# The messages of a graph layer: the scaling and shift of v on GpSimd in place of ScalarE

## What is computed

```python
z = jnp.concatenate([node_feats[src], node_feats[dst], edge_feats], axis=1)
z = z @ W.T + b                                    # 256 columns an edge
mean = jnp.mean(z, axis=0)
var = jnp.mean(jnp.square(z - mean), axis=0)
z = (z - mean) * jax.lax.rsqrt(var + BN_EPS) * gamma + beta
msg = jax.nn.sigmoid(z[:, :H]) * jax.nn.softplus(z[:, H:])
agg = jnp.zeros_like(node_feats).at[src].add(msg)
return node_feats + agg
```

## Time and profile before

| | us |
|---|---|
| median of 3 runs | 4397.55 |
| lowest and highest | 4392.38, 4400.34 |
| the profiled execution | 4391.44 |
| its span in the trace | 4389.2 |
| PE busy | 3005.1 (68%) |
| DVE busy | 2808.1 (64%) |
| POOL busy | 2540.0 (58%) |
| ACT busy | 2214.8 (50%) |

### The profile page before, as it was taken

How to read it: one execution, slowest core, us unless ns; L and a number is a source line. 1 busy time by engine, 2 the same in 40 slices (tenths; PEclk the granted TensorE clock), 3 DMA queues, 4 the chain that set the end, 5 groups by cost and what they waited for, 6 DMA issues and landing times. The chain is left out here.

```text
span 4389.2 us, 80992 instructions
## 1 busy us (share of the span) xinstructions
PE 3005.1 (68%) x17430; PEld 2153.3 (49%) x17431; DVE 2808.1 (64%) x7053; ACT 2214.8 (50%) x5936; POOL 2540.0 (58%) x2618
## 2 busy tenths in 40 slices
PE   6866989999989999999996576666233333333341
PEld 3422444444457777777775465666233333333330
DVE  5898989999965545555553788888434344343457
ACT  2412989889866666666664999997100000000011
POOL 0787777777757777777774000000477777777750
PEclk8998999999999999999998789888655655565555
DMA  6333333333348888888888544442322222222240
GB/s 131 120 91 94 107 101 99 101 101 99 97 123 264 263 263 263 263 263 261 262 264 204 204 175 189 186 173 96 64 52 52 53 52 52 52 53 52 52 30 29
DMA packets 311349, 598.09 MB, mean 136 GB/s; under 512 B 53534, under 2 KB 191943, under 8 KB 305575
## 3 DMA queue, kind: packets, MB, share of 16 engines
q0 software_dynamic: 96992, 228.88, 20.5%
q1 hardware_dynamic: 175480, 246.10, 18.1%
q10 hardware_dynamic: 38736, 121.78, 7.3%
HBM read 406.57 MB, written 189.99 MB: 136 GB/s over the span
## 5 line engine op out<-in xcount | busy, mean ns | idle before, releaser
L345 POOL DMA_INDIRECT rec_d<-arena x830 | 846.7, 1020 | 392.7 <-issue 360.4
L1254 POOL DMA_INDIRECT arena<-x_tab,arena x880 | 834.1, 948 | 323.1 <-issue 278.2
L784 POOL DMA_INDIRECT arena<-b_tab,arena x880 | 832.7, 946 | 304.5 <-issue 256.9
L1266 PE MATMUL psum<-arena 128*128 128x129 f32 x1760 | 413.4, 428 | 730.5 <-DMA arena<-x_tab,arena 717.9
L1266 PEld LDWEIGHTS psum<-arena 128*128 128x128 f32 x1760 | 383.3, 330 | 760.4 <-issue 760.4
L1291 DVE TENSOR_TENSOR arena<-psum,arena 128x129 f32 x880 | 257.5, 293 | 673.0 <-PE psum L1266 553.6
L717 PE MATMUL psum<-arena 128*128 128x440 f16 x3360 | 663.6, 351 | 8.6 <-ACT arena L432 8.4
L805 DVE TENSOR_TENSOR arena<-psum,arena 128x512 f32<-128x512 f32 x440 | 283.4, 686 | 549.7 <-DMA arena<-b_tab,arena 280.3
L897 PE MATMUL psum<-weT,arena 128*128 128x256 f32 x1760 | 547.8, 393 | 53.7 <-DVE arena L805 50.4
L1242 ACT ACTIVATE arena<-l_idx 128x8 int32 (+1 forms) x110 | 22.9, 208 | 1079.1 <-DMA arena<-x_tab,arena 1069.4
L432 ACT ACTIVATE arena<-arena 128x128 f16<-128x128 f16 x1680 | 561.7, 386 | 0.0
(11 more groups left out here) (203 smaller groups left out, 5205.4 us busy)
## 6 DMA issues: line engine op xcount, KB each, us to landing
z_d<-arena ACTq DMA_DIRECT2D x220, 512.0 KB
arena<-z_d SPq DMA_DIRECT2D x44, 2560.0 KB, 8.5
arena<-rec_d SPq DMA_DIRECT2D x220, 260.0 KB
arena<-in_edge_attr SPq DMA_DIRECT2D x83, 640.0 KB
arena<-b_tab,arena POOLq DMA_INDIRECT x880
arena<-x_tab,arena POOLq DMA_INDIRECT x880, 2.5
rec_d<-arena POOLq DMA_INDIRECT x831, 2.6
b_tab<-arena ACTq DMA_DIRECT2D x49, 128.0 KB
```

The costliest lines, as they stand in the source:

```text
L345: nc.gpsimd.indirect_dma_start(rec_rows, bass.IndirectOffsetOnAxis(e_idx[:, s, k:k + 1], 0), e_buf[:, s, k, :], None).then_inc(s_es[s], 16)
L784: nc.gpsimd.indirect_dma_start(bg[:, s, k, :], None, b_tab, bass.IndirectOffsetOnAxis(rec[:, s, k, H:H + 1].bitcast(I32), 0)).then_inc(s_b ...
L1254: nc.gpsimd.indirect_dma_start(xg[:, s, k, :], None, x1_tab, bass.IndirectOffsetOnAxis(gi[:, s, k:k + 1], 0)).then_inc(s_xg[s], 16)
L1266: last = nc.tensor.matmul(bank(4 * s + q)[:, a * 256:a * 256 + H + 1], hotg[:, s, 2 * q + a, :], xg[:, s, 2 * q + a, :], start=True, stop= ...
```

## The change

GpSimd gets a list in the messages block: for each chunk it waits for q of that chunk and then computes s v + t in place over the same 5 x 512 columns with one tensor_scalar, a multiplication and an addition with a scalar per partition. ScalarE's two operations a pair are gone; its wait for both q stays, now ahead of the first logarithm. VectorE's wait for `s_v` stays as it was.

```diff
+            @block.gpsimd
+            def _(pool):
+                def scaled(c, j, it):
+                    v = chunk_half(j, 1)
+                    pool.wait_ge(s_q, c + 1)
+                    settle(pool, s_turn)
+                    nc.gpsimd.tensor_scalar(v, v, bn_s[:, 1:2], bn_t[:, 1:2], ALU.mult, ALU.add).then_inc(s_v, 1)
+
+                chunks(pool, scaled)
+
...
                     for i in range(2):
-                        v = chunk_half(j + i, 1)
                         wait(act, s_q, c + (i + 1))
-                        nc.scalar.activation(v, v, ACT.Identity, bias=bn_t[:, 1:2], scale=bn_s[:, 1:2]).then_inc(s_v, 1)
-                    for i in range(2):
                         nc.scalar.activation(ex[:, i, :, :], ex[:, i, :, :], ACT.Ln, bias=stat[:, 6:7]).then_inc(s_lg, 1)
```

## The result

The change makes the kernel slower by 0.6%: 4423.03 us (median of 5 runs, 4415.92 to 4424.93) against 4397.19 us (5 runs), a ratio of 1.0059 with a 95% interval of 1.0044 to 1.0073, or +19 to +32 us. The profiled execution has a span of 4413.8 us, 24.6 more than before. The forecast was +46 us, with a range from -5 to +132; sign and mechanism came out as forecast, the size at a little over half.

A forecast was written before the change was run, and what follows sets the result against it. ScalarE was taken to bound the messages stage at 28.63 us a pair, VectorE 10% behind. 21 periods x (31.04 - 28.63) = +50.6 us, less 4.9 at the start, gave +45.7: 4443 us, range 4393 to 4530.

The forecast's parts named there:

- Step 1: ScalarE in the messages stage loses two scalings, 4.92 us a pair; at most 2.1 won, plus 4.9 once at the start.
- Step 2: ScalarE's wait ahead of the logarithm, for one less sigmoid, was already satisfied and costs nothing.
- Step 3: GpSimd's operation between second sigmoid and L1027 has 11.4 us of slack, so as a link it costs nothing.
- Step 4: GpSimd's tensor_scalar over 2560 columns takes 3.2 us, within bounds of 2.17 to 5.06 us.
- halved two-input rate: Alternative price of GpSimd's operation, half its two-input tensor_tensor time: 2.5 us.
- Step 5: VectorE stands while GpSimd runs, except for one add; its pair of chunks becomes 31.04 us.
- two small terms: In VectorE's pair: 0.60 us off for one add beside GpSimd; 1.30 us of TensorE waits hidden under the stalls.
- Rival A: VectorE's compares run on beside GpSimd, only operations with two SBUF inputs stall: -49 us, 4349 us; chance 0.16.
- Rival B: GpSimd's operation takes only 2.2 us, the stall eating ScalarE's gain: +2 us, 4400 us; chance 0.09.
- Rival C: Stalls lower TensorE's clock, adding 6.6 us of waits a pair, 138 us over the forecast; chance 0.03.

The follow-up runs named there:

- e2: e1 plus GpSimd's tensor_scalar over 2560 columns on a buffer of its own that nobody waits for: 4418.45 us, 1.0045 of the kernel before.
- e4: The change with GpSimd's operation cut into five pieces of 512 columns: 4397.01 us, 0.9999 of the kernel before.
- e8: The change with GpSimd's operation cut into ten pieces of 256 columns: 1.0051 of the kernel before, 1.0039 when run again.
- e3: e2 with a GpSimd memset of the 2560 columns in place of the tensor_scalar: 4407.35 us, 1.0025 of the kernel before.
- e1: The change without GpSimd's operation and VectorE's wait for it, v left unscaled: 4360.05 us, 0.9914 of the kernel before.
- e6: e1 with the scaling of v as a tensor_scalar on VectorE ahead of L1027: 1.0198 of the kernel before.
- e12: e2 with GpSimd's operation started at the end of L1027's operation, beside VectorE's multiplication, instead of after the sigmoid: 1.0011 of the kernel before.

## Why the prediction came out as it did

*Step 1, ScalarE stops being the bound:* right. VectorE's wait for the logarithm is gone but for the first of the stage, where it fell from 24.32 to 19.62 us, the 4.9 us reckoned (4.7).

*Step 2, the wait before the logarithm:* right, ScalarE is idle for 0.3 us in all before the logarithms, as before the change.

*Step 3, no cost as a link in the chain:* right, shown by e2, which has the cost without the link, and L1034 waited for GpSimd nowhere.

*Step 4, GpSimd's duration, was mis-sized:* 3.2 us forecast, 2.53 measured. This alone is 2 x 0.67 x 21 = 28 us too much. The halved two-input rate, named there and passed over for the middle of the bounds, gave the right 2.5 us, but by luck: the pieces of e4 and e8 show 0.84 ns a column and 0.33 us an operation, not 0.99 ns a column. 0.84 ns is the memset's rate, (5.37 - 2.23) / (6321 - 2560) = 0.835 ns from the earlier trace rows and e3. So the branch of step 4 in which an operation with one input pays once for what it costs over a memset had the right form, and only its 0.12 us was too small: 2.48 - 2.23 = 0.25 us. The estimate from the Trainium skill's line rate ("GPSIMD Engine Reference", Engine selection), 2.13 us, was 0.4 too short for the whole operation, but its 0.83 ns a column agrees with the 0.84. The one from the same page's 1.8 cycles (Elementwise — side-by-side cycle accounting), 3.84 us, was 1.3 too long.

*Step 5, VectorE stands while GpSimd runs:* right in kind, shown by e2 and by the rows of one meeting. Its two small terms were off in opposite directions. An operation costs 1.67 us, not its whole duration once and the duration less 0.60 the other time: of 2.53 us 0.86 are free on the mean, an add or a wait that would have been there anyway. With the measured duration the rule of step 5 gives 2 x 2.53 - 0.60 = 4.46 us a pair, and 3.33 were measured, 24 us too much over the stage. And the waits for TensorE did not go under the stalls; 28.0 us of idle time before the adds are left in the stage, 1.27 a pair, where they were forecast at zero, 27 us too little. These two cancel by luck, so that the miss of 25 us looks like that of the duration alone. With the measured numbers, the 1.67 and 1.27 read from this same trace, the step's sum closes: 25.24 + 2 x 1.67 + 1.27 = 29.85 us a pair. The trace has (3055.88 - 2429.14) / 21 = 29.84 between the first and the last L1034 of a pair's first chunk. 21 x (29.84 - 28.63) - 4.7 = +20.7, and the stage grew by 20.9.

The first and last of these rows:

```profile
2429.14 2.83 DVE L1034 SCALAR_TENSOR_TENSOR arena<-arena 128x2560 f32<-128x2560 f32 x1 [19.62 <-ACT arena L996]
...
3055.88 2.81 DVE L1034 SCALAR_TENSOR_TENSOR arena<-arena 128x2560 f32<-128x2560 f32 x1
```

One reading ahead of the steps was off and changed nothing: the 3.43 us before L1027 end the pair before the one that was added up. The wait that belongs to that pair is the next:

```profile
2715.70 2.82 DVE L1027 SCALAR_TENSOR_TENSOR arena<-arena 128x2560 f32<-128x2560 f32 x1 [2.07 <-ACT arena L989]
```

*Rival A, the compares run on:* false, the compares are what stands; the price of its outcome, -49 us, was also too good by 11, as e1 shows. *Rival B, no change:* near in duration (2.53 against 2.32 us) but outside it. *Rival C:* not as priced. The clock did fall, from 0.88 to 0.84, but the idle time before the adds is 28.0 us against 27.6; its price shows in e6.

The rule of the Trainium skill ("SBUF — State Buffer", Who interferes with whom), that the operation which issues second is blocked to the end of the first, holds in each meeting shown: the compares behind GpSimd, GpSimd behind the multiplication in e12, the free adds from PSUM. That a memset stops the compares (e3) agrees with it as well, as compares of the two-port kind; that they are of that kind was inferred from the rate of a longer tensor_scalar and not shown by itself. That longer one is stopped by a memset as well (4.99 us instead of 3.36, e2).

## What to carry to other kernels

An idle GpSimd is not free help for a VectorE that is nearly full: before moving work there, look for one place in the trace where the two run at once, and charge VectorE the operation's duration less what of VectorE's list can run beside it. Only then compare with the slack that the engine relieved leaves, here 28.63 - 27.09 = 1.5 us a pair against 3.3. If the work must go there, five pieces in place of one took back 26 us in one test, but ten did not, as each has a cost of its own. A start where VectorE would have waited anyway left the stage 24 us shorter in another, compared across groups of runs.

## What the runs showed of the hardware that was not expected

- A GpSimd memset, which reads nothing, stops VectorE's short tensor_scalar compares almost as a tensor_scalar does: four of them took 2.12 us instead of 0.86 (e3).
- Five pieces of 512 columns took 4.21 us on GpSimd where one operation over the 2560 took 2.52, while VectorE lost 1.03 us a chunk instead of 1.67 ((235.0 - 189.7) / 44): of GpSimd's 1.7 us more, 1.3 are also there beside an idle VectorE, 3.79 against 2.48 us (e4).
- GpSimd's tensor_scalar with two scalars per partition, beside no VectorE operation, took 2.48 us for 2560 columns, 0.76 for 512 and 0.54 for 256: as an estimate 0.84 ns a column and 0.33 us an operation (the change, e4, e8).
- A memset of 2.23 us on GpSimd stretched VectorE's tensor_scalar over 6272 columns from 3.36 to 4.99 us (e2).
- VectorE's tensor_scalar over 5 x 512 columns with two scalars per partition took 1.88 us, where 3.36 us for 6272 contiguous ones gave 1.45 (e6). Whether the five rows or the scalars are the reason was not tried.
